# Weights first on the image loads' queue, and no wait ahead of image 0: a convolution kernel on one core

## The chip, the core and the metric

One NeuronCore of one Trainium2 chip runs the whole kernel. The metric is the device time of one execution in microseconds; three runs of the kernel before gave 82.94, 83.00 and 83.01, a median of 83.0. Further, one execution was recorded by the hardware profiler.

## The reference, cut to what matters

For an input of 8 images with 32 channels of 128 x 128 points, in float32:

```python
def reference(x, weight, bias):          # x (8, 32, 128, 128), weight (32, 32, 3, 3)
    return x + conv(group_norm(x, 16), weight, bias)
```

`group_norm` takes mean and variance over 2 channels by 128 x 128 points. `conv` is written with FFTs of size 256 and cuts its output from an offset of 64, so only a corner of each image receives the convolution; in the rest the reference adds the bias alone. Input and output are 16.8 MB each.

## The kernel before, in words

The host splits each image by row and column parity, so that 4 parities by 32 channels fill the 128 partitions, and an image is 64 x 64 values per partition (16 KB, 2 MB in all). Two images form a pair in one tile, `pairs[k]`. Every load and store goes through `Queues`, a small helper that writes one instruction to one engine together with the semaphore waits that its `needs` call for. Instructions of one engine run in the order in which the program writes them; there is no scheduler.

**Loads (lines 181 to 200).** `load` issues one transfer on one queue, with a semaphore of its own. The weights and the bias lie in one small array `wb` (32 rows of 496 values), loaded into `wb_sb` from ScalarE's queue (line 186). Then GpSimd fills the one-column constant `eps` (line 188), and SyncE's queue takes eight loads: image 0 in two halves of 1 MB, images 1 to 3, the pair 4 and 5, and the pair 6 and 7 in two pieces. The first half of image 0 carries a wait for `eps_ok`, so all image loads begin after that memset.

**Setup.** GpSimd builds the averaging matrix `avg` (lines 217 to 239), clears `w_sb` (line 478) and spreads the weights into it (lines 482 and 486), which needs `wb_sb`. ScalarE's first calculation is `warm` (line 241), which reads `eps` and brings in a table of functions.

**Work on an image.** TensorE takes an estimate of the mean (`pilot`, line 269), ScalarE turns it into an origin (line 297) and sums squares (line 308), VectorE sums values (line 287), TensorE adds over the group (line 323), and a short exchange of ScalarE and VectorE (lines 335 to 352) gives the scale. ScalarE writes the normalized corner `g` (line 378), TensorE multiplies it in 3 chunks by 4 products (line 417), VectorE adds the result to the image (line 433), and GpSimd adds the bias elsewhere (line 399). The statistics of later images run under the products of the current one. `keep_warm` (line 457) gives TensorE six products whose results nobody reads, during image 0.

**Stores (line 442).** SyncE's queue issues the stores after all loads, pair by pair, then image by image; image 7 goes in two pieces, of which the last waits for the last addition. One piece of the first pair goes through GpSimd's queue.

Of the kernel before, what the change touches and what calls it, by code (L numbers as in the profile page):

```python
# [153 lines left out]
def conv_preact_kernel(nc: bass.Bass, x: bass.AP, wb: bass.AP, out: bass.AP):  # L154
# [11 lines left out]
    def sbuf(name, *shape):  # L166
        return nc.alloc_sbuf_tensor(name, list(shape), F32).ap()
# [4 lines left out]
    put = Queues(nc)  # L172

    pairs = [sbuf(f"x{pair}", P, 2, H, W) for pair in range(NPAIR)]
    xts = [pairs[img // 2][:, img % 2] for img in range(B)]


    wb_sb = sbuf("wb_sb", *wb.shape)
    loaded = {}

    def load(to, of, *needs, by="sp"):
        name = f"load{len(put.sems)}"
        put.semaphore(name)
        return put(by, lambda e: e.dma_start(to, of), *needs, adds=name)

    weights_in = load(wb_sb, wb, by="act")
    eps = sbuf("eps", P, 1)
    eps_ok = put("pool", lambda e: e.memset(eps, EPS * FFT * FFT), mark=True)  # L188
    loaded[0] = []
    for half in range(2):  # L190
        rows = slice(half * H // 2, (half + 1) * H // 2)
        loaded[0].append((rows.stop, load(xts[0][:, rows, :], x[0, :, 0, rows, :], eps_ok)))
    for img in range(1, 4):
        loaded[img] = [(H, load(xts[img], x[img // 2, :, img % 2]))]
    loaded[4] = loaded[5] = [(H, load(pairs[2], x[2]))]
# [283 lines left out]
    for q in range(4):  # L479
        rin, cin = q // 2, q % 2  # L480
        to = slice(q * C, (q + 1) * C)
        bias_ok = put("pool", lambda e: e.tensor_copy(bias_sb[to, :], wb_sb[:, 15 * C : 15 * C + 1]), weights_in, mark=True)
        for dc, c, b in places[cin]:
# [6 lines left out]
                w_zero, weights_in, mark=True,  # L490
# [11 lines left out]
        adds="moved",  # L502
# [42 lines left out]
    xt, to = xts[B - 1], out[NPAIR - 1, :, 1]  # L545
# [59 lines left out]
```

How the kernel before makes its waits and increments, by code:

```python
    def __call__(self, name, emit, *needs, mark=False, adds=None):  # L68
# [9 lines left out]
            self.done[name] += 1  # L78
            return {**seen, name: self.done[name]}, name
        waits = {}
        for token, of in needs:
            if seen.get(of, 0) < token[of]:
                waits[of] = max(waits.get(of, 0), token[of])
        for token, of in needs:
            self._learn(name, token)
        waits = list(waits.items())
        for of, value in waits[:-1]:
            engine.wait_ge(self.sems[of], value)
        op = emit(engine)
        if waits:
            of, value = waits[-1]
# [2 lines left out]
            of, by = adds, LANDED  # L94
        elif mark:
            of, by = name, int(mark)
        else:
            return None
        op.then_inc(self.sems[of], by)
        self.done[of] += by
        return {**seen, of: self.done[of]}, of
# [7 lines left out]
    def emit_loop(self, times, steps):  # L109
# [26 lines left out]
            at[of] = first  # L136
            engine.reg_mov(values[of], at[of])
        begin = dict(at)
        with engine.Fori(0, times):
            for place in range(size):
                emit, _, mark = rounds[0][place]
                for of, value in plan[place].items():
                    if value != at[of]:
                        engine.reg_add(values[of], values[of], value - at[of])
                        at[of] = value
                    engine.wait_ge(self.sems[of], values[of])
                op = emit(engine)
                if mark:
                    op.then_inc(self.sems["pe"], 1)
```

## Time and profile before

| what | value |
|---|---|
| median of 3 runs | 83.0 us |
| profiled execution | 83.14 us |
| its span, first to last instruction | 81.9 us |
| TensorE busy | 68.3 us (83%) |
| VectorE busy | 50.2 us (61%) |
| ScalarE busy | 47.9 us (58%) |
| GpSimd busy | 31.6 us (39%) |
| moved by DMA | 33.62 MB, mean 410 GB/s over the span |
| SyncE's queue, share of the 16 DMA engines | 96.1% |
| ScalarE's queue, share of the 16 DMA engines | 0.4% |

The profiled execution took 1.24 us outside its span and was 0.14 us above the median. In the views, SP is SyncE, ACT ScalarE, DVE VectorE, POOL GpSimd, PE TensorE and PEld its weight loads; a q behind the name means the engine's instruction queue, where transfers are issued. "L184" is line 184. Times count from the first instruction of the span.

### The profile page before, as it was taken

To read this page: it belongs to the slowest core of one execution; us is meant where nothing else is said; L and a number is where in the kernel's file an instruction comes from. 1 tells how busy PE (TensorE), PEld (TensorE's weight loads), DVE (VectorE), ACT (ScalarE), POOL (GpSimd) and SP (SyncE) were. 2 spreads that over 40 slices of the span, in tenths; PEclk is the share of its full clock that TensorE was granted. 3 is DMA by queue.
4 is the path that set the end of the run, shared out by engine and by line. 5 is a ranking of instruction groups with operands and counts; after the bars stand their busy time and mean duration, and the time that the engine had idled before them with its cause. 6 is when DMAs were issued, how large, how long until landed. Compare 5 with 4: busy or idle time off the path is not lost.

```text
span 81.9 us, 685 instructions
## 1 busy us (share of the span) xinstructions
PE 68.3 (83%) x222; PEld 42.0 (51%) x222; DVE 50.2 (61%) x43; ACT 47.9 (58%) x53; POOL 31.6 (39%) x43
## 2 busy tenths in 40 slices
PE   0009979999999999999999999999999999996000
PEld 0006354556666666576666666666666666662000
DVE  0009936960699499949968994997799416003300
ACT  3306957990599479749957992996699460000000
POOL 6994000004069910104997860292068009400000
PEclk9999999999999999999999999999999999999995
DMA  0999999999979989999897998969969999999996
GB/s 17 330 408 460 464 400 440 440 416 440 536 336 464 480 368 410 429 390 468 374 550 336 488 454 337 518 288 512 496 272 488 408 392 480 408 400 480 373 408 260
DMA packets 2308, 33.62 MB, mean 410 GB/s; under 512 B 312, under 2 KB 346, under 8 KB 644
## 3 DMA queue, kind: packets, MB, share of 16 engines
q1 hardware_dynamic: 2164, 33.36, 96.1%
q0 software_dynamic: 96, 0.19, 0.7%
q10 hardware_dynamic: 48, 0.06, 0.4%
HBM read 16.84 MB, written 16.78 MB: 410 GB/s over the span
## 4 chain that ended last, share of the span: by engine, by line
PE 79%; DMA 6%; ACT 5%; DVE 2%; issue 1%; POOL 0%; POOLq 0%
PE ps L417 73%; DMA x<-x_dram 6%; ACT unused L308 5%; PE ps L457 2%; PE ps_m L323 2%; DVE x L433 2%; PE ps_w L269 1%; ACT origin L297 0%; POOL eps L188 0%; POOL pair L217 0%; POOLq L590 0%
## 5 line engine op out<-in xcount | busy, mean ns | idle before, releaser
L417 PE MATMUL ps<-g,w_sb 128*128 128x363 f32 (+1 forms) x192 | 61.1, 475 | 0.0
L417 PEld LDWEIGHTS ps<-g,w_sb 128*128 128x128 f32 x192 | 36.2, 195 | 20.1 <-issue 1.8
L287 DVE TENSOR_REDUCE sums<-x 128x1 f32<-128x4096 f32 x7 | 30.9, 4410 | 0.4 <-DMA x<-x_dram 0.4
L399 POOL TENSOR_SCALAR x<-x,bias_sb 128x1984 f32<-128x1984 f32 (+3 forms) x12 | 23.2, 1941 | 18.7 <-ACT origin L297 14.4
L308 ACT ACTIVATE unused<-x,origin 128x4096 f32<-128x4096 f32 (+1 forms) x9 | 30.0, 3330 | 0.3
L433 DVE SCALAR_TENSOR_TENSOR x<-ps,bias_sb,x 128x1089 f32<-128x1089 f32 (+2 forms) x9 | 10.9, 1220 | 7.7 <-PE ps L417 7.7
L378 ACT ACTIVATE g<-x,rstd 128x1089 f32<-128x1089 f32 (+2 forms) x8 | 9.4, 1188 | 3.4 <-DVE rstd L352 3.4
L287 DVE TENSOR_REDUCE first_sums<-x 128x1 f32<-128x2048 f32 x2 | 4.6, 2285 | 6.2 <-DMA x<-x_dram 6.2
L262 POOL COPY sums<-x 128x1 f32<-128x1 f32 x6 | 1.0, 184 | 18.7 <-DMA x<-x_dram 15.2
L340 DVE TENSOR_SCALAR var<-ps_m,square 128x1 f32<-128x1 f32 x8 | 1.7, 218 | 8.9 <-ACT square L335 8.9
L335 ACT ACTIVATE square<-ps_m,origin 128x1 f32<-128x1 f32 x8 | 2.1, 261 | 7.7 <-PE ps_m L323 7.7
L269 PE MATMUL ps_w<-x,avg 128*128 128x1 f32 x4 | 1.1, 355 | 6.1 <-DMA x<-x_dram 6.1
L457 PE MATMUL ps<-x,avg 128*128 128x512 f32 x6 | 5.8, 1108 | 0.0
L269 PEld LDWEIGHTS ps_w<-x,avg 128*128 128x128 f32 x4 | 1.0, 310 | 7.5 <-POOL w_sb L486 6.1
L323 PEld LDWEIGHTS ps_m<-sums,avg 128*128 128x128 f32 x16 | 2.8, 189 | 2.2 <-DVE x L433 1.0
L346 ACT ACTIVATE std<-var,eps 128x1 f32<-128x1 f32 x8 | 2.4, 295 | 2.3 <-DVE var L340 2.3
L349 DVE RECIPROCAL rstd<-std 128x1 f32<-128x1 f32 x8 | 1.3, 164 | 2.9 <-ACT std L346 2.9
L297 ACT ACTIVATE origin<-ps_w 128x1 f32<-128x1 f32 x2 | 0.3, 160 | 4.0 <-PE ps_w L269 4.0
L486 POOL COPY w_sb<-wb_sb 32x128 f32<-32x128 f32 (+1 forms) x8 | 2.5, 339 | 0.0
L323 PE MATMUL ps_m<-sums,avg 128*128 128x3 f32 x16 | 2.3, 215 | 0.0
L457 PEld LDWEIGHTS ps<-x,avg 128*128 128x128 f32 x6 | 1.8, 334 | 1.0 <-issue 1.0
L323 PEld LDWEIGHTS ps_m<-first_sums,avg 128*128 128x128 f32 x4 | 1.2, 324 | 1.7 <-ACT unused L308 1.1
(21 smaller groups left out, 13.8 us busy)
## 6 DMA issues: line engine op xcount, KB each, us to landing
x<-x_dram SPq DMA_DIRECT2D x3, 2048.0 KB, 15.4
out_dram<-x SPq DMA_DIRECT2D x3, 2048.0 KB
x<-x_dram SPq DMA_DIRECT2D x1, 4096.0 KB, 28.9
out_dram<-x SPq DMA_DIRECT2D x1, 4096.0 KB
out_dram<-x SPq DMA_DIRECT2D x1, 3904.0 KB
x<-x_dram SPq DMA_DIRECT2D x1, 3328.0 KB, 36.3
x<-x_dram SPq DMA_DIRECT2D x2, 1024.0 KB, 6.1
out_dram<-x SPq DMA_DIRECT2D x1, 1056.0 KB
```

The lines of the kernel that those rows point to most:

```text
L269: "pe", lambda e: e.matmul(ps_w[:, img : img + 1], avg, xts[img][:, 0, 0:1], start=True, stop=True),
L287: lambda e: e.tensor_reduce(to_sum(img, k)[:, 0:1], piece, mybir.AxisListType.X, ALU.add),
L308: lambda e: e.activation(unused[:, rows.start * W : rows.stop * W], piece, AF.Square, bias=origins[img], accum_out=to_sum(img, k)[:, 1:2],),
L323: lambda e: e.matmul(ps_ms[:, 0 : of.shape[1]], avg, of, start=(part == 0), stop=(part == last)),
L335: lambda e: e.activation(squares[img], ps_ms[:, 0:1], AF.Square, bias=origins[img]),
L346: lambda e: e.activation(stds[img], variances[img], AF.Sqrt, bias=eps, scale=float(FFT * FFT)),
L378: lambda e: e.activation(g[:, rows, :], xt[:, LO + rows.start : LO + rows.stop, LO:W], AF.Identity, bias=rstd[:, 1:2], scale=rstd[:, 0:1],),
L399: put("pool", lambda e: e.tensor_scalar(part, part, 1.0, bias_sb, op0=ALU.mult, op1=ALU.add), *free, mark=mark)
L417: lambda e, k=k, dc=dc, rows=rows, top=top: e.matmul(ps[:, 0:rows, 0 : N - dc], w_sb[:, k * P : (k + 1) * P], g[:, top : top + rows, dc:N] ...
L433: lambda e: e.scalar_tensor_tensor(part, in0=ps, scalar=bias_sb, in1=part, op0=ALU.add, op1=ALU.add),
L457: "pe", lambda e: e.matmul(pss[1][:, 0, :], avg, piece, start=True, stop=True),
L486: lambda e: e.tensor_copy(w5[to, :, dc, :, c.start * C : c.stop * C], taps[:, 1 - rin : 5 - rin, b, :].rearrange("p (dr r) b o -> p dr r ( ...
```

## The change

The load of the weights becomes the first entry of SyncE's queue, ahead of image 0. The wait for GpSimd's memset is taken off the first half of image 0, and ScalarE's queue issues no transfer any more. The memset of `eps` stays, and `warm` on ScalarE still waits for it.

```diff
-    def load(to, of, *needs, by="sp"):
+    def load(to, of):
         name = f"load{len(put.sems)}"
         put.semaphore(name)
-        return put(by, lambda e: e.dma_start(to, of), *needs, adds=name)
-
-    weights_in = load(wb_sb, wb, by="act")
+        return put("sp", lambda e: e.dma_start(to, of), adds=name)
+
     eps = sbuf("eps", P, 1)
     eps_ok = put("pool", lambda e: e.memset(eps, EPS * FFT * FFT), mark=True)
+    weights_in = load(wb_sb, wb)
     loaded[0] = []
     for half in range(2):
         rows = slice(half * H // 2, (half + 1) * H // 2)
-        loaded[0].append((rows.stop, load(xts[0][:, rows, :], x[0, :, 0, rows, :], eps_ok)))
+        loaded[0].append((rows.stop, load(xts[0][:, rows, :], x[0, :, 0, rows, :])))
```

The order on SyncE's queue at the start of the program, before (`x` are the images, `wb_sb` the weights and the bias):

```order
L184 DMA x<-x_dram 128x2048 x2
L184 DMA x<-x_dram 128x4096 x3
L184 DMA x<-x_dram 128x8192
L184 DMA x<-x_dram 128x6656
L184 DMA x<-x_dram 128x1536
```

and with the change:

```order
L184 DMA wb_sb<-wb_dram 32x496
L184 DMA x<-x_dram 128x2048 x2
L184 DMA x<-x_dram 128x4096 x3
L184 DMA x<-x_dram 128x8192
L184 DMA x<-x_dram 128x6656
L184 DMA x<-x_dram 128x1536
```

The weights are one row ahead of everything, and the image loads follow in the same order as before.

ScalarE's first instructions before:

```order
L184 DMA wb_sb<-wb_dram 32x496
L241 ACT_TABLE_LOAD
L241 ACTIVATE warm<-eps 128x1
L297 ACTIVATE origin<-ps_w 128x1
L308 ACTIVATE unused,first_sums<-x,origin 128x2048 x2
```

and with the change:

```order
L241 ACT_TABLE_LOAD
L241 ACTIVATE warm<-eps 128x1
L297 ACTIVATE origin<-ps_w 128x1
L308 ACTIVATE unused,first_sums<-x,origin 128x2048 x2
L335 ACTIVATE square<-ps_m,origin 128x1
```

The transfer is gone from ScalarE, and its table load comes first. TensorE, VectorE and GpSimd keep their order.

## Rows read from the trace of the kernel before

**Rows 1.** The page: busy tenths of the DMA engines in 40 slices.

```profile
DMA  0999999999979989999897998969969999999996
```

**Rows 2.** Windows: stretch, length, GpSimd's `wb_sb` reads, TensorE clock, DMA share, GB/s.

```profile
1.70:1.80 0.10, 0.00 (x0) 1.00 0.00 0
1.80:1.90 0.10, 0.00 (x0) 1.00 0.91 139
...
2.30:3.00 0.70, 0.00 (x0) 1.00 0.50 152
...
3.00:81.00 78.00, 3.00 (x12) 0.99 1.01 428
...
77.00:81.00 4.00, 0.00 (x0) 0.81 1.02 427
```

**Rows 3.** Timeline: start, duration, engine, line; the issues at the start and end.

```profile
0.81 0.40 ACTq L184 DMA_DIRECT2D wb_sb<-wb_dram  x1
0.81 0.10 POOL L188 MEMSET eps<- 128x1 f32 x1 [0.29 <-POOLq L590]
...
0.93 0.38 SPq L184 DMA_DIRECT2D x<-x_dram  x1
...
1.24 1.28 ACT L241 ACT_TABLE_LOAD   x1 [1.24 <-PEq L590]
...
1.37 0.42 SPq L184 DMA_DIRECT2D x<-x_dram  x1
...
76.51 0.33 SPq L442 DMA_DIRECT2D out_dram<-x  x1
```

**Rows 4.** Chain that ended last: start, length, what; its beginning, one image, its end.

```profile
0.93 5.07 DMA x<-x_dram
...
6.14 0.57 PE ps_w L269 x2
...
6.73 0.18 ACT origin L297
...
6.94 4.09 ACT unused L308 x4
...
13.57 0.39 PE ps_w L269 x2
...
20.50 7.22 PE ps L417 x24
...
75.00 1.48 DVE x L433 x2
```

**Rows 5.** SyncE's waits: line, releaser, total us, times, longest.

```profile
SPq L563 <- DMA out_dram<-x: 5.0, 1, 5.0
...
SPq L184 <- POOL pair L217: 0.3, 1, 0.3
```

**Rows 6.** DMA issues on the page: count, KB each, us from issue to landing.

```profile
x<-x_dram SPq DMA_DIRECT2D x2, 1024.0 KB, 6.1
...
wb_sb<-wb_dram ACTq DMA_DIRECT2D x1, 62.0 KB, 2.1
```

**Rows 7.** DMA packets begun up to 2.1 us: queue, packets, MB, share.

```profile
q10 hardware_dynamic: 25, 0.05, 10.7%
```

**Rows 8.** DMA packets begun from 2.1 to 3.0 us.

```profile
q1 hardware_dynamic: 21, 0.17, 87.0%
q10 hardware_dynamic: 23, 0.02, 12.5%
```

**Rows 9.** Timeline of the first readers of the weights and of the images.

```profile
3.94 0.18 POOL L482 COPY bias_sb<-wb_sb 32x1 f32<-32x1 f32 x1
...
6.03 2.29 DVE L287 TENSOR_REDUCE first_sums<-x 128x1 f32<-128x2048 f32 x1 [6.03 <-DMA x<-x_dram]
...
6.48 0.63 POOL L486 COPY w_sb<-wb_sb 32x256 f32<-32x256 f32 x2
...
13.36 4.42 DVE L287 TENSOR_REDUCE sums<-x 128x1 f32<-128x4096 f32 x1 [0.37 <-DMA x<-x_dram]
```

## The prediction

> **What bounds the kernel now.** I read the page's slices first, since the kernel moves 33.62 MB and little is left of 83 us once they are moved. The DMA engines are full from the second slice to the end [rows 1]. The windows make that exact: from 3 to 81 us their share is 1.01 at 428 GB/s [rows 2], so no stretch after the start is free in which a late byte could be caught up. The end agrees. The last store, 1056 KB or 1.08 MB, is issued at 76.51 [rows 3], yet from 77 to 81 us the engines still move 4.0 x 427 = 1.71 MB [rows 2]. So 0.63 MB of earlier stores, 1.5 us of work, was still ahead of it half a microsecond after its issue, and SyncE's last wait of 5.0 us [rows 5] is mostly a queue.
>
> The chain of waits gives a second bound beside that one. Image 0's first half is issued at 0.93 and holds the chain for 5.07 us; then come the pilot on TensorE, ScalarE's origin and squares, the group sums, the pilot of image 1, and from there TensorE's products, 7.22 us per image with no gap for a load, up to the last addition at 75.00 [rows 4]. This chain has some slack against the DMA stream: by the 1.5 us above, the last store could have been issued about 1 us later and still found work ahead of it.
>
> Both bounds hang on the same point: when image 0 begins to flow. A shift there moves the DMA stream as a whole, because nothing in it is idle, and moves the chain as a whole, because its first link is that transfer. VectorE's first sum too starts at 6.03 as the first half lands, and its first whole-image sum at 13.36 as image 1 lands [rows 9]. So the question is by how much the image stream starts later or earlier, and that shift goes into the time at full size.
>
> **The change, part by part.**
>
> *The wait for GpSimd's memset goes.* ScalarE issues the weights at 0.81, and GpSimd begins the memset at 0.81 too, right after the common barrier; SyncE issues at 0.93 [rows 3]. Its wait is put down to GpSimd with 0.3 us [rows 5], most of which is the barrier itself. I take it that SyncE without the wait begins as ScalarE does, at 0.81. That alone is worth 0.93 - 0.81 = 0.12 us.
>
> *The weights are issued by SyncE.* ScalarE spends 0.40 us on that issue [rows 3]; SyncE's issues of the much larger image halves take 0.38 and 0.42, so the price hardly depends on size and I take 0.40. Between two of SyncE's issues lie 1.37 - 0.93 - 0.38 = 0.06 us. So image 0 is issued at 0.81 + 0.40 + 0.06 = 1.27 in place of 0.93: **0.34 us later**. The other seven image loads move by as much, but they queue behind full engines and that costs nothing by itself.
>
> *What the engines do meanwhile.* The issue is not yet the flow. By 2.1 us the packets of the weights' queue that have begun are 25 of its 48, 0.05 MB, and none of an image [rows 7]. From 2.1 to 3.0 us 21 image packets and the other 23 weight packets begin side by side [rows 8]. Those 21 image packets fill 87.0% of 16 engines for 0.9 us, 0.60 us each, where an 8 KB packet at 428 GB/s over 16 engines takes 0.31 us. That is 0.29 x 21 / 16 = 0.38 us lost per engine, part to sharing with the weights, part to the first reads being slow for any reason. With the change the weights' packets have their engines to themselves, in the time for which image 0 is not issued yet.
>
> What this gives back isn't in the trace. Its lower bound is nothing: the first image packet follows its issue by the same delay as before. Its upper bound is all of the 0.38, and in addition the difference between the two first-packet delays: the first traffic, the weights', appears between 1.80 and 1.90 [rows 2], about 1.04 us after their issue at 0.81, while the image's first packets come at 2.1 at the earliest [rows 7, 8], 1.17 after 0.93; the difference is 0.13 us, if the image waited for the weights there. So between 0 and 0.51 us. I take 0.15, the engines' own time for the weights, 0.0635 MB at 428 GB/s: that work stood ahead of and among the first image packets, and now lies in the gap. It is nearer to the lower end, because 25 of the 48 weight packets were under way before any image packet came, and because 0.51 would be over three times the engine time that the weights need.
>
> The Trainium skill's page "DMA: Bandwidth & Descriptors", section "Queues, rings and completion order", says that each DMA engine takes turns between the queues that have work, packet by packet. The trace agrees in so far as packets of both queues begin in the same stretch [rows 8]; by this rule the two loads did share the engines before, and some of the 0.38 us belongs to that.
>
> *The weights land no later.* They take 2.1 us from issue to landing [rows 6] and would land at about 2.9 as before. GpSimd first reads them at 3.94, once it has built its matrix and cleared `w_sb`, without a wait, and ends spreading them at about 7.1 [rows 9], while the first product that needs them follows the pilot of image 1 at 13.57 [rows 4]. A microsecond of lateness would be covered by GpSimd's setup.
>
> *ScalarE loses an issue.* Its table load can begin at about 0.8 in place of 1.24 [rows 3]; the work after it waits for the pilot until 6.73 [rows 4]. Worth nothing.
>
> **The sum.** +0.34 - 0.15 = +0.19, rounded to **+0.2 us** on the image stream, the chain and the end. The profiled execution would go from 83.14 to 83.34; it stands 0.14 above the median of the runs, which goes from 83.0 to **83.2**.
>
> **The rivals.**
>
> *The whole issue counts.* If first reads are slow for their own reasons, nothing comes back, and the stream shifts by 0.34; with an issue or a gap that is somewhat longer on SyncE, by 0.4. That gives 83.3 to 83.4. For it: from 6.03 to 13.36 [rows 9] the 3.15 MB of the second half and of image 1 land, 429 GB/s, the rate of the whole stream, so the start alone decides. Against it: the two queues' packets do overlap now. The Trainium skill's page "DMA: Bandwidth & Descriptors", section "Issuing engines are not separate DMA queues", states the rule that speaks against this change: all queues run on the same engines, and issuing from several saves the sequencer's time of issue. By that rule the image loses the time of the issue, the 0.34 above, and this rival is the outcome; no row of the kernel before shows the two ways of issuing side by side.
>
> *The start-up is fixed.* Full rate begins at about 3.0 us; from 2.3 to 3.0 the engines begin only 152 GB/s worth [rows 2]. If what decides is when the weights are off the engines, then image packets that come 0.34 later find them free and lose nothing. The shift is then within 0.1 of zero: 83.0.
>
> *Faster: the slowest engine is freed.* A load is waited for until all 16 of its counts are in (`LANDED` in the code), so its slowest share decides. If the engines that finish last are those on which image packets stood among weight packets, putting the weights wholly ahead takes that delay away. The most it can give back is the 0.51 above, so the shift is 0.34 - 0.51 = -0.17 and the time 82.83, about 82.8. It decides for this side only if more than 0.34 of that 0.51 was the weights' doing. Against it: the weights are 0.15 us of engine time in all.
>
> *The change doesn't do what it says.* If SyncE reaches its first issue only at 0.93 whatever the memset does, the image is issued at 0.93 + 0.46 = 1.39, and the shift is 0.31 after the same 0.15: 83.3. The simultaneous start of ScalarE and GpSimd speaks against it.
>
> **How the numbers follow.** A change of this kernel's time by less than about 0.2%, 0.17 us, cannot be told from none. I give the forecast, a shift of 0.1 to 0.3, 0.40; the whole issue counting, with the late SyncE, 0.25; the fixed start-up, 0.22; the freed engine, 0.13. Over 83.17 lie the second and some six tenths of the first: 0.25 + 0.24, about 0.49. Faster by over 0.17 is the last case, 0.13. Between lies 0.38. The range runs from 82.85, just inside the last case, to 83.40, a shift of 0.4 with the whole issue; it leaves out about 0.15.
>
> **What would show it.** In the profile of the changed kernel, SyncE's first issue should stand at 0.8 and image 0's at 1.27; the first sum on VectorE should begin at about 6.2 and image 1's sum at about 13.55; TensorE's products should keep 7.2 us per image; the last addition should start at about 75.2 and the engines should be full from 3.2 to 81.2. The sum is wrong if the first half lands within 0.1 of 6.03 (the start-up was fixed), before 5.9 (the weights had held it up), or at 6.35 and later (nothing came back). The whole argument is wrong if the first landing moves and the end does not: then a gap that I don't see in the stream takes up the shift.

## The result and the profile after

The changed kernel takes **83.59 us** (median of 6 runs, 83.45 to 83.79), against 83.0 before; the ratio is 1.0071, 95% interval 1.0056 to 1.0086. It is 0.59 us slower. The forecast was 83.2 and its range ended at 83.40: the direction was right, the size was not.

The profiled execution took 83.67 us, its span 82.3. The beginning of its timeline (start, duration, engine, line), with the first readers of images 0 and 1:

```profile
0.81 1.28 ACT L241 ACT_TABLE_LOAD   x1 [0.81 <-PEq L590]
...
0.81 0.39 SPq L184 DMA_DIRECT2D wb_sb<-wb_dram  x1
...
1.26 4.16 SPq L184 DMA_DIRECT2D x<-x_dram  x8
...
3.94 0.18 POOL L482 COPY bias_sb<-wb_sb 32x1 f32<-32x1 f32 x1
...
6.39 2.29 DVE L287 TENSOR_REDUCE first_sums<-x 128x1 f32<-128x2048 f32 x1 [6.39 <-DMA x<-x_dram]
...
13.72 4.42 DVE L287 TENSOR_REDUCE sums<-x 128x1 f32<-128x4096 f32 x1 [0.58 <-DMA x<-x_dram]
```

The issue of image 0 stands at 1.26, 0.33 later than in [rows 3], and both first sums are 0.36 later than in [rows 9]. The weights' first reader stays at 3.94.

The windows from 3 to 81 us and at the end (columns as in [rows 2]):

```profile
3.00:81.00 78.00, 3.00 (x12) 0.97 1.00 426
77.00:81.00 4.00, 0.00 (x0) 0.79 1.02 425
```

SyncE's last wait, and the end of the chain of waits:

```profile
SPq L563 <- DMA out_dram<-x: 5.5, 1, 5.5
```

```profile
74.92 0.03 issue
74.94 1.48 DVE x L433 x2
```

The stream is as full as before, while the last addition starts at 74.94, 0.06 earlier than in [rows 4] although the images came later. So the chain through TensorE did not carry the loss; the transfers did. The span grew by 0.4, from 81.9 to 82.3, and 0.36 of that is there at the first landing. These are figures of one pair of executions; further down, a second profile of the kernel before has its first landing 0.3 us earlier, so the medians of several runs have to decide.

The other part is not in the span. Before, an execution took 1.24 us more than its span; the six of the changed kernel took 1.35 to 1.43 more, on average 1.38. (A time outside the span is the run's time less its span, which is known to 0.1 us, so a single one is uncertain by 0.05. The later runs of the kernel before lie at 1.18 to 1.29, with means of 1.23 to 1.25.)

### The profile page after: what moved, and what is told of

It reads as the page before. It is cut to its first block, busy times and chain, and to the rows that moved or that the text cites. A ratio compares the mean times of both kernels' runs of the same rounds, so it can differ in the third digit from the quotient of the medians.

```text
span 82.3 us, 685 instructions
## 1 busy us (share of the span) xinstructions
PE 66.8 (81%) x222; PEld 41.2 (50%) x222; DVE 50.2 (61%) x43; ACT 47.9 (58%) x53; POOL 31.6 (38%) x43
## 4 chain that ended last, share of the span: by engine, by line
PE 74%; DMA 14%; DVE 2%; SPq 1%; issue 0%
PE ps L417 73%; DMA x<-x_dram 14%; DVE x L433 2%; SPq L184 1%; PE ps_m L323 1%; PE ps_w L269 0%
## 5 line engine op out<-in xcount | busy, mean ns | idle before, releaser
L457 PE MATMUL ps<-x,avg 128*128 128x512 f32 x6 | 4.9, 942 | 0.0
L352 DVE TENSOR_SCALAR rstd<-ps_m,rstd 128x1 f32<-128x1 f32 x8 | 1.8, 219 | 0.3
```

The lines of the kernel that those rows point to most:

```text
L352: lambda e: e.tensor_scalar(rstds[img][:, 1:2], ps_ms[:, 0:1], rstds[img][:, 0:1], -1.0, op0=ALU.mult, op1=ALU.mult),
L457: "pe", lambda e: e.matmul(pss[1][:, 0, :], avg, piece, start=True, stop=True),
```

## The experiments

They asked three things: what in the span costs 0.4, whether the image stream alone sets the end, and what lengthens the time outside. The theory to test (A) was that the time follows the issue of image 0 one to one; the first rival (B) that the weights' place ahead in the same queue is the cost. Each median is in the table behind them, with its ratio to runs of the kernel before made beside it; these have medians of 82.89 to 82.96 and a median span of 81.7.

**The wait alone.** no_wait takes only the wait for GpSimd away.

```diff
-        ... load(xts[0][:, rows, :], x[0, :, 0, rows, :], eps_ok)))
+        ... load(xts[0][:, rows, :], x[0, :, 0, rows, :])))
```

> The kernel before with the wait for GpSimd's memset alone taken off; the weights stay on ScalarE's queue. Theory A, the time follows the issue of image 0 one to one: image 0 issued at 0.81 in place of 0.93, first sum on VectorE at 5.9 in place of 6.03, 82.9 us. Theory B, what counts is that the weights are off the engines before the images come: first sum at 6.0 or a little later, since now both issues start together, 83.0 to 83.1 us.

It is slower: 83.3 us, ratio 1.0042 (1.0026 to 1.0058). The timeline and the issues of its profile (in the issues: count, KB each, us from issue to landing):

```profile
0.81 0.41 ACTq L184 DMA_DIRECT2D wb_sb<-wb_dram  x1
...
0.81 4.08 SPq L184 DMA_DIRECT2D x<-x_dram  x8
...
6.04 2.29 DVE L287 TENSOR_REDUCE first_sums<-x 128x1 f32<-128x2048 f32 x1 [6.04 <-DMA x<-x_dram]
```

```profile
x<-x_dram SPq DMA_DIRECT2D x2, 1024.0 KB, 6.2
...
wb_sb<-wb_dram ACTq DMA_DIRECT2D x1, 62.0 KB, 3.7
```

Issued 0.12 earlier, image 0 lands no earlier, and the weights need 3.7 us in place of 2.1 [rows 6]. Both theories miss the time, A by 0.4 us and B by 0.2 to 0.3; the median span is 82.1, 0.4 over before. Theory A falls for issues ahead of 0.93. Why the earlier issue loses, and not only fails to gain, no run shows.

**The image first, the weights behind.** weights_late gives them to ScalarE behind `warm` (its queue issues them at 0.95, not at the expected 2.3); weights_second to SyncE, between the two halves; weights_twice is weights_late with a second, unread copy.

```diff
+    # weights_late, behind the activation of warm
+    weights_in = load(wb_sb, wb, by="act")
+    # weights_second, behind the first half of image 0
+    weights_in = load(wb_sb, wb)
+    # weights_twice, behind the load of weights_late
+    copy_in = load(wb_copy, wb, by="act")
```

> Image 0 first on SyncE's queue at 0.81 without a wait, the weights on ScalarE's queue behind its table load and first activation, at about 2.3. The weights then share the engines with a full stream of images and land at about 5 to 6; GpSimd spreads them until about 9, under image 0's statistics. Theory A: 82.8 us, faster than before by the 0.12 of the issue. Theory F (some packets of the weights must be ahead for the image stream to start quickly, or: whichever load goes first pays the start-up): first sum at 5.7, but the stream behind it not earlier than in the run without the wait, 83.2 to 83.3 us.

> All on SyncE's queue without a wait, ScalarE's unused as in the change, but the weights are issued between the two halves of image 0. Theory A: image 0 issued at 0.81, first sum at 5.9, and the DMA stream begins 0.12 us earlier than before; the weights land at about 6.1, GpSimd spreads them from there until about 9.3, which image 0's statistics cover; span about 81.8, and 82.9 us, or 83.0 if the unused queue costs 0.13 outside the span (theory C). Theory B: the weights now stand behind the first half, so image 0 lands earlier than in every other version, 5.8 or less, 82.8 us.

> The kernel with image 0 first at 0.81 and the weights on ScalarE's queue at 0.95, and behind them a second copy of the weights on the same queue, which nobody reads. Theory H (weights that go inside the full image stream cost their engine time there, 0.15 us at 428 GB/s or up to 0.3, while before they went ahead of it for nothing): 83.23 plus 0.15 to 0.3, 83.4 to 83.5 us. If the loss of the versions with the image first is all in the start-up: 83.25 us.

Medians 83.23, 83.64 and 83.79: none is faster. weights_second misses both of its theories by over 0.6 us. weights_twice lies 0.3 over theory H; it has 1.56 outside its span where weights_late has 1.21. weights_late's timeline:

```profile
0.81 3.96 SPq L184 DMA_DIRECT2D x<-x_dram  x8
...
0.95 0.38 ACTq L184 DMA_DIRECT2D wb_sb<-wb_dram  x1
...
5.88 2.29 DVE L287 TENSOR_REDUCE first_sums<-x 128x1 f32<-128x2048 f32 x1 [5.88 <-DMA x<-x_dram]
```

The first sum stands 5.07 us after the issue here, 4.90 after it in weights_second and 5.13 in weights_twice. Where the image follows the weights by 0.12 it stands 5.10 after it [rows 3, 9], 4.80 in a second profile of the kernel before and 4.91 in before_more_act. So an image that opens the transfers lands no sooner behind its issue than one that follows. And then the weights lie inside the stream: from the first sum to the end of the span these profiles take 76.2, 76.3 and 76.3 us, against about 76.0 in most kernels with the weights ahead (table). The time of weights_late is that of theory F, the first sum is not (5.88 for 5.7). Theory H is not shown: its sign fits these three profiles, and a second copy added 0.2 to the median span, but after_more_act, with the weights ahead, takes 76.3 as well.

**The delay alone.** delay_short, delay_only and delay_long leave the weights with ScalarE and let image 0 wait for an added memset of 128 x 128, 384 and 1280 values (here delay_only's).

```diff
+    delay = sbuf("delay", P, P * 3)
+    delay_ok = put("pool", lambda e: e.memset(delay, 0.0), mark=True)
-        ... x[0, :, 0, rows, :], eps_ok)))
+        ... x[0, :, 0, rows, :], delay_ok)))
```

> The kernel before, where image 0 waits for an added GpSimd memset of 128 x 128 values, so that it is issued at about 1.07 in place of 0.93. Theory A (slope one from 0.93): +0.14, 83.08 us. Theory G (what counts is that the image's packets arrive while the weights' are still on the engines; missing that costs a fixed 0.15 to 0.2 and slope one after it): 83.2 to 83.3 us.

> The kernel before, where image 0 waits for one more GpSimd memset (128 x 384 values, not used) in place of the small one, so that SyncE issues image 0 at about 1.27 as in the changed kernel, with no transfer ahead of it on its queue and the weights on ScalarE's. Theory A (the time follows the issue of image 0): +0.34, first sum at 6.2 to 6.4, 83.25 to 83.3 us. Theory B (the weights' place in the same queue is the cost, the delay is not): 82.9 to 83.0 us.

> The same with a memset of 128 x 1280 values, image 0 issued at about 2.0, 1.07 later than before; GpSimd's setup and weights end about 1.2 later, still under image 0's statistics. Theory A: slope one, 84.0 us. Theory G: a fixed 0.15 to 0.2 more, 84.2 us. A slope of 1.5, as the run with 0.36 of delay and 0.54 of loss would have it: 84.5 us.

Issued at 1.08, 1.29 and 2.04, thus 0.15, 0.36 and 1.11 later than before, they lose 0.08, 0.53 and 0.97 us. That excludes theory B: a delay costs without any change of queue. It is close to slope one at the two ends; the middle one lies 0.17 above it, and its interval, 0.41 to 0.66, leaves the 0.36 out. Theory G, a fixed loss on top of slope one, fails at both ends. delay_long's timeline:

```profile
2.04 4.10 SPq L184 DMA_DIRECT2D x<-x_dram  x8
...
6.71 2.29 DVE L289 TENSOR_REDUCE first_sums<-x 128x1 f32<-128x2048 f32 x1 [6.71 <-DMA x<-x_dram]
```

This run also shows the start of image 0 with no neighbour at all, since the weights, issued at 0.81, land 1.8 us later, at 2.6. The packets that begin from 2.9 to 3.9 us, with the share of 16 engines:

```profile
DMA packets 21, 0.17 MB, mean 172 GB/s; under 512 B 0, under 2 KB 0, under 8 KB 0
q1 hardware_dynamic: 21, 0.17, 81.7%
```

These are the first 21 image packets, as many as in [rows 8], and they take 0.817 x 16 x 1.0 / 21 = 0.62 us each, against 0.60 there beside the weights.

In delay_short TensorE ran ahead, and this settles what sets the end. Its chain and SyncE's last wait:

```profile
73.36 1.48 DVE x L435 x2
```

```profile
SPq L565 <- DMA out_dram<-x: 6.5, 1, 6.5
```

The last addition starts 1.64 us earlier than in [rows 4], and the span is 81.7, as in the median execution of the kernel before: the time saved turned into a longer wait for the stores, 6.5 us in place of 5.0 [rows 5].

**The issue without the bytes.** tiny_ahead keeps the weights with ScalarE, drops the wait and puts a load of 1 KB, which nobody reads, ahead of image 0.

```diff
+    scratch = sbuf("scratch", 16, 16)
+    small_in = load(scratch, wb[0:16, 0:16])
```

> Weights on ScalarE's queue as before, no wait, and on SyncE's queue a load of 1 KB (16 rows of 16 values) ahead of image 0, whose data nobody reads. Theory A (the issue of a transfer ahead is the cost, whatever its size): image 0 issued at 1.27, first sum at 6.4, span 82.2 to 82.3; the time is 83.4 if the rest of the loss stems from ScalarE's queue standing unused, 83.6 if not. Theory B (the weights' bytes ahead of the image in one queue are the cost): 1 KB costs nothing, first sum at 6.0, 83.0 us.

83.29 us, ratio 1.0042 (1.0025 to 1.0059): 1 KB costs 0.37, as the issue, not the bytes, would have it. The first sum of this profile stands at 6.03, earlier than the 6.4 expected, and its span at 82.0; the median span is 82.05, 0.35 over before, and the time is 0.1 under the expected 83.4. The sharpest comparison is with act_used, described below: there the two loads have changed places, the weights' 62 KB ahead of image 0 and 1 KB on ScalarE's queue. It takes 83.31 us with a median span of 82.1. So the weights ahead in the same queue neither cost more than 1 KB there nor give anything back.

**The wait within the change.** keep_wait is the changed kernel with `eps_ok` kept.

> The changed kernel with the wait for GpSimd's memset kept on image 0. The memset ends at 0.91, while image 0 is issued at 1.26 behind the weights, so in every theory by which the wait's removal is idle in this change: 83.6 us, span 82.2, outside 1.38. If the wait matters by itself: 83.4 or less.

83.48 us, ratio 1.0062 (1.0049 to 1.0075), outside 1.33 to 1.41: as the change itself, its interval overlapping, and image 0 is issued at 1.26 as there. Behind the weights' issue the wait is idle.

**The time outside.** act_used and act_late are the changed kernel with an unread 1 KB load on ScalarE's queue, as its first instruction and behind `warm`.

> The changed kernel, with a load of 1 KB on ScalarE's queue as its first instruction, whose data nobody reads; so ScalarE's queue is in use again, while the weights stay first on SyncE's queue. The changed kernel's time outside the span was 1.37 us in its profile, against 1.24 before. Theory C, the unused queue lengthens the time outside the span: span 82.3 as changed, outside back to 1.24, 83.45 us. Theory D, the time outside doesn't depend on the queue: 83.6 us as changed.

> The changed kernel, with a load of 1 KB on ScalarE's queue behind the table load and the first activation, at about 2.3, whose data nobody reads. Theory C (a queue of ScalarE's that is not used at all lengthens the time outside the span): time outside the span 1.24, span as changed, 83.4 us. Theory C2 (what counts is that ScalarE's table load comes first, at 0.81): outside 1.37 as changed, 83.6 us. If the use of ScalarE's queue at the start also brought the image stream forward in the run with 1 KB on it at 0.81, the first sum here is at 6.35 as changed.

They return to 1.24 and 1.25 outside, and in act_late the table load still comes first, so its order is not the cause. (act_late's load is issued at 0.95, not at 2.3.) Theory C seemed to hold, until weights_twice, with two transfers on ScalarE's queue, showed 1.34 to 1.88. Three more runs part the transfers from the instructions: after_more_act and before_more_act add a second small activation behind `warm` to the changed kernel and to the one before, act_two adds two 1 KB loads to the changed one.

```diff
+    warm2 = sbuf("warm2", P, 1)
+    put("act", lambda e: e.activation(warm2, eps, AF.Sqrt))
```

> The changed kernel with one more small activation on ScalarE and still no transfer on its queue. Theory C (the number of transfers on ScalarE's queue sets the time outside the span): outside 1.33 to 1.43 as changed, 83.55 us. Theory I (the number of ScalarE's instructions, which the change lowers by one, sets it): outside 1.19 to 1.29, 83.4 us.

> The kernel before with one more small activation on ScalarE, the weights still on its queue. Theory C: outside 1.19 to 1.29, 82.95 us. Theory I: outside 1.33 or more, 83.1 us.

> The changed kernel with two loads of 1 KB on ScalarE's queue, whose data nobody reads; one such load had brought the time outside the span back to 1.25, two loads of the weights had it at 1.34 to 1.88. If the count of one is what is special: outside 1.33 or more. If any use of the queue is enough and the larger values came from the weights' bytes: outside 1.19 to 1.29, 83.4 us.

after_more_act, with no transfer at all, has 1.20 to 1.28 in its five runs; before_more_act, with its transfer as before, has 1.31 to 1.89 in nine. Theory C falls; theory I fits these two. Kernels with as many ScalarE instructions as the kernel before, transfers counted, lie at 1.18 to 1.29, those with one less at 1.33 to 1.43, those with one more at 1.28 to 1.36 (act_two) or 1.31 to 1.89 (before_more_act, weights_twice). act_two thus lies between its two expectations. So the time outside does not simply fall or rise with the number, only three numbers were tried, and whether the number itself counts or something that goes with it is not shown. after_more_act takes 83.54 us all the same and not 83.4, since its spans, 82.0 to 82.5, came out longer. before_more_act loses 0.26 us for an idle activation of 0.2 us, with its median span unchanged at 81.7.

**The kernel before again**, for what two samples differ by.

> The kernel before, unchanged, for a second profile and for what two samples of one kernel differ by. All theories: the ratio to before is 1.000 within 0.002; span 81.5 to 81.9, first sum on VectorE between 5.8 and 6.05.

Ratio 0.9996 (0.9986 to 1.0005). Its profile has the first sum at 5.73, the one shown ahead of the prediction at 6.03: single executions differ by 0.3 us at the first landing.

| kernel | image 0 issued | first sum | span, profile | difference | median us | ratio | median span | mean outside |
|---|---|---|---|---|---|---|---|---|
| before (profile shown) | 0.93 | 6.03 | 81.9 | 75.9 | 83.0 | | | 1.24 |
| before_again | 0.93 | 5.73 | 81.8 | 76.1 | 82.89 | 0.9996 | 81.7 | 1.24 |
| before_more_act | 0.93 | 5.84 | 81.8 | 76.0 | 83.15 | 1.0036 | 81.7 | 1.47 |
| delay_short | 1.08 | 5.72 | 81.7 | 76.0 | 83.04 | 1.0010 | 81.8 | 1.23 |
| delay_only | 1.29 | 6.17 | 82.3 | 76.1 | 83.47 | 1.0065 | 82.25 | 1.23 |
| delay_long | 2.04 | 6.71 | 82.7 | 76.0 | 83.93 | 1.0124 | 82.7 | 1.25 |
| tiny_ahead | 1.26 | 6.03 | 82.0 | 76.0 | 83.29 | 1.0042 | 82.05 | 1.23 |
| changed | 1.26 | 6.39 | 82.3 | 75.9 | 83.59 | 1.0071 | 82.2 | 1.38 |
| keep_wait | 1.26 | 6.10 | 82.1 | 76.0 | 83.48 | 1.0062 | 82.1 | 1.37 |
| act_used | 1.26 | 6.07 | 82.1 | 76.0 | 83.31 | 1.0045 | 82.1 | 1.24 |
| act_late | 1.26 | 6.11 | 82.1 | 76.0 | 83.37 | 1.0058 | 82.1 | 1.25 |
| act_two | 1.26 | 6.75 | 82.7 | 76.0 | 83.54 | 1.0073 | 82.2 | 1.32 |
| after_more_act | 1.26 | 6.25 | 82.5 | 76.3 | 83.54 | 1.0068 | 82.3 | 1.24 |
| no_wait | 0.81 | 6.04 | 82.1 | 76.1 | 83.30 | 1.0042 | 82.1 | 1.22 |
| weights_late | 0.81 | 5.88 | 82.1 | 76.2 | 83.23 | 1.0043 | 82.0 | 1.21 |
| weights_second | 0.81 | 5.71 | 82.0 | 76.3 | 83.64 | 1.0093 | 82.25 | 1.39 |
| weights_twice | 0.81 | 5.94 | 82.2 | 76.3 | 83.79 | 1.0116 | 82.2 | 1.56 |

The column of differences is the finding on the span: whatever a kernel does, its end stands 75.9 to 76.3 us behind its first landing, most often 76.0. The four with the weights inside the image stream, at the foot of the table, lie at 76.1 to 76.3, but so does after_more_act. No version beats the kernel before.

## Why the prediction was wrong

**What held.** The DMA stream sets the end, a shift of its first landing goes into the span at full size, and the chain through TensorE has slack (delay_short, and the column of differences). The issue went to 1.26 where 1.27 was forecast. The weights landed in time, and ScalarE's table load cost nothing in the span. The Trainium skill's page "DMA: Bandwidth & Descriptors", section "Issuing engines are not separate DMA queues", says that issuing from several engines saves only the time of the issue. These runs agree: a load ahead of image 0 on SyncE's queue loses 0.37 us with 1 KB (tiny_ahead) and 0.39 with the weights' 62 KB (act_used).

**The first step that failed** is the term of -0.15 us, the engines' time for the weights that was to come back. It did not: in the pair of profiles the first sum moved by 0.36 for an issue 0.33 later, and by the median spans the change loses 0.5. The reason given was that the first image packets were slow because weights ran beside them. In the changed kernel they have the engines almost to themselves. The packets that it began from 2.25 to 3.15 us, with their queue's share of 16 engines:

```profile
DMA packets 19, 0.13 MB, mean 146 GB/s; under 512 B 3, under 2 KB 3, under 8 KB 3
q1 hardware_dynamic: 19, 0.13, 74.8%
```

Three are under 512 B, the other 16 are image packets: 0.748 x 16 x 0.9 / 16 = 0.67 us each, no better than the 0.60 of [rows 8], where weights began beside them. In delay_long, where no weight is left, the same 21 packets as there take 0.62. The slow start belongs to the image load itself; of the 0.38 us that the prediction counted as lost per engine, no part can be seen to come from the weights. So the rival by which the whole issue counts was the right one for the span. The rival of freed engines fails with the same rows, and the fixed start-up, by which the span would not have grown, fails with the median spans.

Two smaller readings failed beside it. The 0.12 us for the wait's removal was not there to be had: SyncE does begin at 0.81 in the changed kernel, but the weights carry no wait, and with the wait kept image 0 is issued at 1.26 too (keep_wait); taken away alone, it costs 0.4 (no_wait). And the chain did not move with the stream: the last addition starts at 74.94 where 75.2 was forecast.

**The second step that failed** is one that was not written down as such: carrying the change of the span over to the median with the time outside held at 1.24. It rose by 0.14, as the change takes one instruction from ScalarE; with an idle activation in its place (after_more_act) the time outside is back at 1.24. No term, rival or bound had a place for that; with it the rival's 83.34 becomes 83.48, which already leaves the range.

**What stays open.** 0.34 and 0.14 make 0.48 of the 0.59, whose own interval is 0.46 to 0.71. The median spans of the eight kernels with image 0 issued at 1.26 to 1.29 lie 0.35 to 0.6 over the 81.7 before, on average 0.46, some 0.1 more than the issue accounts for, while delay_long loses 1.0 in its span for 1.11 and delay_short 0.1 for 0.15. In time delay_long loses 0.14 less than its issue, about the size of the failed term, but its interval, 0.90 to 1.14, has the whole 1.11 inside, so it shows no credit either. One execution's landing scatters by 0.3, and no run singles this remainder out. Why the time outside the span goes with the number of ScalarE's instructions is open as well; nothing in a profile shows that stretch.

## What to carry to other kernels

Where the DMA engines never idle, as here, the kernel's span is its first large landing plus a constant, so a transfer issued ahead of that one on the same queue costs its issue, here about 0.4 us, for 1 KB as for 62 KB. Of the places tried for the small load, the one on another queue, 0.12 us ahead of the large one, was the best. Do not credit a start-up loss to a neighbour without a row in which the neighbour is absent. And before effects of a few tenths are read from a time, subtract the span from it: this kernel loses 0.1 to 0.3 us outside it by one instruction more or less on ScalarE.

## What the runs showed of the hardware that was not expected

- The first 8 KB image packets take 0.62 us each even alone (delay_long), against the 0.31 that an 8 KB packet takes at the stream's 428 GB/s. The first 1 MB load needs 4.6 to 5.5 us from issue to its first reader, while the next megabyte's reader starts 2.4 us after that one (8.47 against 6.03 in the kernel before).
- Issuing the image 0.12 us earlier, together with the weights, stretches the weights' landing time from 2.1 to 3.7 us and brings the image no gain. A wait that looks idle kept the two 0.12 us apart, and taking it away cost 0.38 us (no_wait).
- The time outside the span goes with ScalarE's number of instructions: 1.21 to 1.25 us on average with as many as the kernel before, 1.37 to 1.39 with one less, 1.32 to 1.56 with one more, whether the instruction is a transfer or an activation.
